# Turned rows moved beside the last tile of two attentions, and longer filling groups at three places, in a four-layer decoder kernel

## The reference, cut to what matters

```python
x = x + jnp.tanh(g_xattn[0]) * _L0_xattn_ref(_layernorm(x, axis=-1), ctx_1024, ctx_1024, ...)
x = x + jnp.tanh(g_ffn[0])   * _L0_ffn_ref(_layernorm(x, axis=-1), L0_ffn_router_w, ...)   # top-1 of 8 experts
x = x + jnp.tanh(g_xattn[1]) * _L1_xattn_ref(_layernorm(x, axis=-1), ...)
x = x + jnp.tanh(g_ffn[1])   * _L1_ffn_ref(_layernorm(x, axis=-1), L1_ffn_gate_w, ...)     # top-2 of 8 experts
x = x + ... # attention with causal scores; latent attention and top-2 experts
x = x + ... # rotary attention; one expert per batch, chosen from the last token
```

## Time and profile before

| | us |
|---|---|
| median of 3 runs | 1002.13 (1001.85 to 1003.92) |
| the profiled execution, its own time | 1003.53 |
| its span, first to last instruction | 1001.8 |
| PE busy (share of the span) | 905.4 (90%) |
| DVE busy | 729.6 (73%) |
| ACT busy | 551.0 (55%) |
| POOL busy | 431.4 (43%) |

### The profile page before, as it was taken

The page is one execution under the profiler, slowest core; times in us unless marked ns, Lnnn a source line. Parts: engine busy times, 40 slices in busy tenths (PEclk is TensorE's granted clock), DMA queues, the critical chain, the costliest instruction groups (busy, mean ns, idle before and its releaser), DMA issues.

```text
span 1001.8 us, 22263 instructions
## 1 busy us (share of the span) xinstructions
PE 905.4 (90%) x7859; PEld 629.1 (63%) x7863; DVE 729.6 (73%) x2035; ACT 551.0 (55%) x1331; POOL 431.4 (43%) x511
## 2 busy tenths in 40 slices
PE   5999887998798999889986898998989999989977
PEld 3777535667698999668774343434436777667764
DVE  5799998996786876789984776766734635479972
ACT  3786355883454556556642276766754243357743
POOL 5113555671265763645458657564531200022120
PEclk9899797997999999999999588989999999999999
DMA  9400000000211122300001322222002000000001
GB/s 334 165 2 3 3 5 1 2 2 1 59 47 40 44 47 76 119 0 1 0 1 55 87 64 82 62 79 58 26 1 106 2 1 1 1 1 3 2 2 43
DMA packets 29829, 40.75 MB, mean 41 GB/s; under 512 B 11456, under 2 KB 25024, under 8 KB 29216
## 3 DMA queue, kind: packets, MB, share of 16 engines
q1 hardware_dynamic: 27232, 34.28, 10.9%
q0 software_dynamic: 2496, 5.16, 2.0%
HBM read 31.45 MB, written 7.82 MB: 39 GB/s over the span
## 4 chain that ended last, share of the span: by engine, by line
PE 37%; issue 7%; POOL 6%; DVE 4%; ACT 3%; SPq 1%; DMA 0%; DVEq 0%; POOLq 0%; ACTq 0%
PE ps L922 5%; PE ps L912 5%; PE ps L1315 5%; PE ps L1287 4%; POOL att L1926 4%; PE ps L1299 4%; PE ps L831 2%; PE ps L840 1%; PE ps L843 1%; PE ps L816 1%; PE ps L1367 1%; PE ps L821 1%; PE ps L1375 1%; PE ps L770 1%; SPq L581 1%
## 5 line engine op out<-in xcount | busy, mean ns | idle before, releaser
L1907 POOL TENSOR_TENSOR rstd<-ve,minus_half 128x4 f32<-128x4 f32 x38 | 39.1, 1036 | 124.1 <-DVE ve L2214 107.5
L2860 DVE CUSTOM_DVE_ANT_0 U<-ps,cmaskb 128x384 bf16<-128x384 f32 (+1 forms) x128 | 53.9, 421 | 43.7 <-PE ps L1287 43.5
L2860 DVE CUSTOM_DVE_ANT_0 C<-ps,cmaskb 128x512 bf16<-128x512 f32 (+1 forms) x128 | 71.0, 555 | 20.1 <-PE ps L1287 17.2
L922 PEld LDWEIGHTS ps<-U,att 128*128 128x128 f32 x512 | 66.4, 191 | 30.4 <-issue 26.3
L1006 PE MATMUL ps<-PT,att 128*128 128x128 f32 x624 | 80.2, 283 | 4.6 <-issue 3.2
L2522 DVE SCALAR_TENSOR_TENSOR U<-ps,w_all,U 128x128 f32<-128x128 f32 x128 | 36.0, 344 | 62.1 <-PE ps L922 62.0
L1006 PEld LDWEIGHTS ps<-PT,att 128*128 128x128 f32 x624 | 75.2, 197 | 8.1 <-issue 5.6
L1577 ACT ACTIVATE att<-ps 128x512 f32<-128x512 f32 x64 | 38.1, 597 | 72.9 <-PE ps L912 72.8
L1299 PE MATMUL ps<-U,W 108*128 108x512 bf16 (+3 forms) x256 | 73.5, 327 | 5.0 <-ACT VW L1837 2.1
L1287 PE MATMUL ps<-W,U 72*128 72x512 bf16 (+3 forms) x256 | 67.7, 340 | 9.9 <-DVE VBD L2860 6.4
L922 PE MATMUL ps<-U,att 128*128 128x128 f32 x512 | 67.6, 276 | 0.6 <-ACT att L1577 0.6
(11 more groups left out here) (471 smaller groups left out, 2471.3 us busy)
## 6 DMA issues: line engine op xcount, KB each, us to landing
U<-in_ffn SPq DMA_DIRECT2D x1, 6176.0 KB, 23.0
U<-split SPq DMA_DIRECT2D x144, 32.0 KB
W<-split SPq DMA_DIRECT2D x144, 32.0 KB
W<-in_packed SPq DMA_DIRECT2D x1, 2162.5 KB, 22.4
U<-in_ffn SPq DMA_DIRECT2D x1, 2060.0 KB, 9.1
U<-in_moe SPq DMA_DIRECT2D x1, 2048.0 KB, 7.4
split<-VBD SPq DMA_DIRECT2D x4, 384.0 KB, 2.8
split<-W SPq DMA_DIRECT2D x4, 384.0 KB, 2.5
```

Of the source, the lines that this page charges most:

```text
L922: t = mm(ps[:, 4 + e % 2, i * D:(i + 1) * D], hh[:, u % 2, i * P:(i + 1) * P], W2M[:, e, j, :], start=(j == 0 and i == 0), stop=(j == J2 - ...
L2860: v.tensor_tensor_reduce(unused[t % 2][:, 0:z], ps[:, 2 * (t % RINGS), 0:z], visible[:, S - z:S], -1.0, -NEG, ALU.add, ALU.min, nm[:, n % ...
```

## The change

In X0 and X1 the rows of the first batches are normalised within the attention's loop (X0: batch 0 before the last `divide`, batches 1 and 2 behind it; X1: batches 0 and 1 before the last `divide`, 2 right behind it), and PE turns batch 0 in its loop behind the last weighted values, in place of filling products. Turned rows go through score banks, one for each of three batches, so that a turn doesn't wait for a copy. Behind the loop PE's order is route 0, turn 1, turn 2, route 1, route 2, ten filling products, turn 3, route 3, and PE and ACT no longer wait for all of x. Filling products in the attentions' tails: X0 17 + 13 before, 10 now; X1 6 + 26 before, none now; 10 more ahead of turn 3 in each. Filling groups elsewhere: `keep_warm` 7 to 9 turns (of eight) at the end of `dispatch` and 12 products more before the second slot's turn in `routed`; 8 to 12 turns in X3; in F3 10 products between L1355 and L1358, and 4 to 7 turns ahead of the experts.

```diff
-AHEAD = 2
+AHEAD = 3
+ROW_BANK = (0, 1, 2, 0)
...
         def turn_bank(s, b):
-            return 5 if s in (X0, F0, F1, MOE, F3) and b % 2 == 1 else 7
+            if s in (F0, F1):
+                return ROW_BANK[b]
+            return 5 if s in (X0, MOE, F3) and b % 2 == 1 else 7
...
+            def turn_row(s, b):
+                pe.wait_ge(s_xn, TB * (ROUND0[s] + b + 1))
+                if b == B - 1:
+                    turned_copied(s, 0)
+                for i in range(TB):
+                    t = pe.transpose(ps[:, ROW_BANK[b], i * P:(i + 1) * P], xn1[:, b * TB + i, 0:D], ident)
+                t.then_inc(turned, 1)
+
+            def other_rows(s, weight):
+                route(s, 0, weight)
+                turn_row(s, 1)
+                turn_row(s, 2)
+                route(s, 1, weight)
+                route(s, 2, weight)
+                warm(10, 3)
+                turn_row(s, B - 1)
+                route(s, B - 1, weight)
... PE, headwise
                     if s == X3 and k == 1:
-                        keep_warm(8)
+                        keep_warm(12)
...
-                    if k == NT + 2:
+                    if k == NT + 2 and s == X3:
                         warm(13, 0)
...
-                        if k == NT + 1:
+                        if k == NT + 1 and s == X0:
+                            pe.wait_ge(shifted, n0 + NT + 1)
+                            turn_row(F0, 0)
+                            warm(10, 3)
+                        elif k == NT + 1:
                             warm(17, 0)
... PE, dispatch and routed
-                keep_warm(7)
+                keep_warm(9)
...
                 for t in range(SLOTS + 2):
+                    if t == 1:
+                        warm(12, 7)
... PE, behind X0, and second_cross
-            prepare(F0, lambda b: route(F0, b, w("0rw")))
+            other_rows(F0, w("0rw"))
...
                     if k == NT + 3:
-                        warm(6, 0)
+                        pe.wait_ge(scores_read, NT + 1)
+                        turn_row(F1, 0)
                     if 0 <= k - 4 < NT:
                         turn_back(k - 4)
-                    if k == NT + 3:
-                        warm(26, 0)
...
-            prepare(F1, lambda b: route(F1, b, w("1gw")))
+            other_rows(F1, w("1gw"))
... PE, F3
             mm(ps[:, 6, 0:B], w("wp1"), FT[:, S - 1:B * S:S], start=True, stop=True).then_inc(pol, 1)
+            warm(10, 5)
             pe.wait_ge(pol_sb, 1)
...
-            keep_warm(4, bank=6)
+            keep_warm(7, bank=6)
... ACT: X0's loop, and behind X0 and X1
+                    if s == X0 and k == NT + 2:
+                        turned_copy(F0, 0, 0, [(FT[:, cols(0)], None, None)])
...
-            starts(act, F0)
-            for b in range(B):
+            for b in range(1, B):
...
-            starts(act, F1)
             for b in range(B):
... POOL, second_cross
-                    if 0 <= k - NT - 1 < EARLY:
-                        root(ROUND0[F1] + k - NT - 1, k - NT - 1)
+                    for b in {NT + 1: (0, 1), NT + 2: (2,)}.get(k, ()):
+                        root(ROUND0[F1] + b, b)
... DVE, headwise and second_cross
+                    if s == X0 and k == NT:
+                        normed_rows(F0, 0)
                 if s == X0:
-                    for n in range(AHEAD):
+                    for n in range(1, AHEAD):
                         normed_rows(F0, n)
...
-                    if 0 <= k - NT < EARLY:
-                        b = k - NT
+                    for b in {NT: (0, 1), NT + 1: (2,)}.get(k, ()):
                         dve.wait_ge(x_new, XNEW0[X1] + (b + 1) * TB)
                         moments(ROUND0[F1] + b, rows_of(x, b), b)
-                for n in range(AHEAD):
-                    normed_rows(F1, n)
+                    for b in {NT + 2: (0, 1), NT + 3: (2,)}.get(k, ()):
+                        normed_rows(F1, b)
```

## The result

The changed kernel took 993.52 us (median of 7 runs, 991.21 to 998.33) against 1002.62 for the kernel before beside it (7 runs, 1000.84 to 1004.70): ratio 0.9908 [0.9891, 0.9925], 9.1 us faster. The prediction said 997.5, from 994.0 to 1001.3: right in sign, too small, and the time lies just under the range.

What follows compares the result with a forecast made beforehand. Bound: PE's queue at half clock in the attention tails (F0's gate by only 0.64 us, then DVE). -0.6 - 2.4 - 0.4 - 1.0 + 0 + 0.3 - 1.9 = -6.0 from 1003.53: 997.5 us, range 994.0 to 1001.3.

Steps and rivals of the forecast that it cites:

- F0's gate: F0: one route instead of two queued behind the last turn, DVE becomes the bound, gate at about 109.7: -0.6 us.
- F1, gate and behind: F1: gate at about 240.7 with half clock from about 235.5, -2.4 us, and -0.4 behind the gate.
- fill before the slots: Before the slots: longer filling keeps the clock full at the slots' start: -1.0 us, between 0 and -1.7.
- X3's group: X3, ahead of the score: 32 more products fit PE's 2.44 us of idling, clock stays full: 0, at most +0.5.
- F3: F3: ten products between the policy products cost +0.3 us; full clock on the first experts' products saves 1.9.
- stages not touched: Stages the change leaves alone: no term in the sum; shifts there named only as a way of being wrong.
- The exponent's 0.4: Behind F1's gate: part of DVE's 0.94 us wait for the exponent goes, late projections and fillers set against it: -0.4 us.
- Rival 2: Clock falls at once in both tails for want of fillers: F0 +0.3, F1 -0.2, total 1001.0 us; chance 0.12.
- Turns and the clock: F3's earlier trace, nearly only turns with full clock behind, was taken to speak against the skill's rule on turns.
- Rival 3: F3's filling group becomes a wait if half clock begins before it, first experts 2.5 us later: 1006.1 us; chance 0.06.
- Rival 4: Clock falls in neither tail: F1's gate at 239.3, projections behind both gates at full clock: 994.2 us; chance 0.10.
- the last step of the sum: Whole kernel: the profiled execution's forecast of 997.5 us was set for the median too, 4.6 below its 1002.13.

Runs made afterwards that it cites:

- E8: Changed kernel with more filling products in both attention tails and 20 products in the fourteenth slot: 993.19 us, ratio 0.9892.
- E11: The same kernel as E8, run again: 991.93 us, ratio 0.9896.
- E13: Changed kernel with 20 products in the fourteenth slot and more filling in F1's tail, F0's tail as changed: 992.20 us, ratio 0.9903.
- E3: Kernel before with one dead DVE reduction, 1.35 us, ahead of F1's gate: 1001.36 us, ratio 0.9979.
- E4: Changed kernel with one dead DVE reduction, 2.02 us, ahead of F1's gate: 996.76 us, ratio 0.9943.
- E5: Changed kernel itself, no edit, run and profiled again: 995.87 us, ratio 0.9932.
- E10: Changed kernel with X3's first filling group back from 12 to 8 turns: 995.34 us, ratio 0.9922, 5 runs.
- E2: Kernel before with the longer filling groups alone (X3, before the slots, F3), row work as before: 1000.02 us, ratio 0.9965.
- E1: Changed kernel with the filling groups as before, so the row work of both attentions alone: 997.61 us, ratio 0.9952.
- E9: Kernel before with X3's first filling group 12 turns instead of 8: 1001.60 us, ratio 0.9982.
- E12: Changed kernel with more filling in both tails, without the fourteenth slot's 20 products but with E8's moved wait for `gi_set`: 995.83 us, ratio 0.9920.
- E6: Kernel before itself, no edit, run and profiled again: 1001.67 us, ratio 0.9995.
- E14: Changed kernel itself, no edit, run and profiled a third time: 996.19 us, ratio 0.9931.
- E7: Kernel before with only the row work of X1 and F1 as changed: 999.10 us, ratio 0.9967.

## Why the prediction was wrong in size

Point by point, by the sum's own terms. "With" and "without" are means over all profiles that have and lack the edit, without E8 and E11 to E13 and, in F1, without the delayed E3 and E4:

| step | forecast | first profile | with - without, all profiles |
|---|---|---|---|
| F0's gate | -0.6 | -0.75 | -0.72 (always -0.75) |
| F1, gate and behind | -2.8 | -2.44 | -2.2 (-1.06 to -3.34) |
| fill before the slots | -1.0 | -1.33 | -0.9 |
| X3's group | 0 | 0 | -1.4 |
| F3 | +0.3 - 1.9 | -1.82 | -1.6 |
| stages not touched | 0 | -6.0 | no difference shown; -5.6 to +4.0 in 320-860 alone |

- *F0*: right, mechanism and size. DVE was the bound; the gate had no idle time before it. The gain is 0.1 over the bound of 0.64 that the text gave.
- *F1*: right in mechanism. The text placed the gate at 240.7 if the clock fell at 235.5 and at 242.9 if at 231. It fell at 233.5 in the first profile (gate 239.22, after an F1 that began 1.37 earlier) and at 231.1 in E5, where the gate gained 1.10 and not 0.2. The early fall was overpriced. The exponent's 0.4 did not come in the first profile. On the mean F1 gave 2.2 of the 2.8.
- *Rival 2*, the fall at once in both tails, happened in E5 and E10: half clock from 101.4 and 101.7 in F0, from 231.1 and 231.4 in F1. The want of fillers isn't shown to be the cause in F0: E2 and E3, which have the old tail, fell at 101.5 and 101.9, and the first and third profile of the changed kernel at 103.8 and 104.3. In F1 no profile with the old tail fell before 234.6. The price in the text was wrong as well. Its terms 3 x 1.71 + 1.07 + 2 x 0.87 from 100.5 come to 108.4 and not to 106.9 for turn 3; in E5, which was 1.1 ahead of the kernel before at this point, turn 3 started at 104.62 and waited for DVE's rows (0.20), not for PE's queue, and the gate came without idle time before it, so F0's gain stayed. E5, turn 3 and the gate of F0, then the gate of F1:

```profile
104.62 1.12 PE L647 MATMUL ps<-W,KBD 128*128 128x128 f32 x4 [0.20 <-DVE KBD L2256]
...
108.46 0.28 DVE L2456 TENSOR_TENSOR att<-ps,W 128x128 f32<-128x128 f32 x1
...
240.02 0.29 DVE L2471 COPY att<-ps 128x128 f32<-128x128 f32 x1 [5.27 <-PE ps L685]
```

- *Turns and the clock*: in the window 230.1 to 233.5 of the first profile PE was busy for 3.20 of 3.40 us, with turns and router products of 8 columns alone, and half clock followed. The Trainium skill ("TensorE: Matmul & The Clock Gate", Part 4) says that a turn doesn't count as a busy PE in the way a product does. This window agrees with it; the window of turns in the earlier trace rows, from which the prediction argued, with full clock behind it, does not. No run here decides it.
- *Fill before the slots*: about as priced, though part of it can come without the group: the entry was 0.8 ahead in E1 and E3 and 1.3 in E9, all with the old group. With the new one it was 1.3 ahead in all six profiles that the table counts, but only 0.6 to 0.8 in E8, E11 and E12, where half clock lay at 259 us.
- *F3*: right; the ten products cost nothing that shows. Rival 3's mechanism did appear once. In E13 half clock lay on the fillers, and the step gave 0.90 instead of 1.82:

```profile
963.46 4.91 PE L621 MATMUL ps<-identb 128*128 128x128 bf16 x56
968.21 1.94 PE L1403 MATMUL ps<-FT,att 128*128 128x512 f32 x4
```

- *Rival 4*, no fall in either tail: its 994.2 takes 0.9 off for the exponent's wait, of which the sum had taken 0.4 already and which was 0.94 in all; it should have been 994.6, and the low end of the range stands on it.

**The step that failed** is the X3 term: "The clock was full here and stays: 0. Bounds: +0.5 [...], and a few tenths less than nothing in runs where the clock fell." showed PE idle for 2.44 us behind 64 fillers. That was the sign, the same as at the slots, where I did price it; I let one profile's full clock overrule it. In five of six executions the clock fell there, and the loss is 0.85 to 2.1 us, no few tenths.

**The second failure** is the last step of the sum. "The median of the runs is 1.4 lower than the profiled one; [...] so I set the same 997.5 for the median": that took the whole difference of two draws off the gain. The changed kernel's terms by the last column add up to 6.8 us, from the median 1002.9 to 996.1. The 20 runs have 994.87 (mean 995.54), which the standard deviation of 3.1 allows. With X3 in and the 1.4 not taken off, the forecast would have been 1002.13 - 6.0 - 1.4 = 994.7.

**The draw.** The first seven runs were lower than the next thirteen (993.52 against 995.87 and 996.19); over all runs the two medians lie 8.0 us apart, so some 1.1 us of the 9.1 is luck, and 994.87 would have been inside the range. My range counted unknown terms of the change and nothing for the spread of the stages it leaves alone; the text named this only as a way of being wrong. It began with the reading of the earlier trace rows: "the rest is full" passed over the 8s at 25 to 50, 575 to 625 and 650 to 675 us, and the slices hide single stretches of 3.4 us, such as those from 271.0, 312.0, 434.9 and 516.8 us. Such stretches are what falls differently from one execution to the next. That the untouched stages took another course in each execution is shown by E5, E6 and E14. What sets where the first half-clock stretch begins (19.5 to 22.6 us in sixteen profiles) stays open.

## What to carry to other kernels

When the clock drops in short stretches, one profile is one draw: profile the same kernel two or three times before pricing a dip, or its absence, at a place where PE waits (2.44 us in X3, 2.6 us in the fourteenth slot). Give every such place a chance of the fall and its price, and don't go by whether the clock happened to fall there once. And compare a new version stage by stage on the instructions of the bounding engine: F0 gave its 0.75 us in every profile that has the edit and F3 its 1.8 in all but one, F1 anything from 1.1 to 3.3 by the table above, and the stages that the change leaves alone moved by as much as the whole gain.

## What the hardware showed that I had not expected

- The same instructions from 320 to 860 us took from 5.6 us less to 4.0 us more than in the first profile, by where half clock fell.
- Half clock can last long on work that another execution runs at full clock: 23.9 us behind X2 in E14, without a break, on work that had 3.4 us of it in the first profile of the kernel and none in E5. That the slower products themselves held the clock down is a reading that no run tests.
- 1.4 us of dead work on the bounding chain cost nothing that can be measured (E3, 0.9979 [0.9959, 0.9998]); in its profile 0.89 of it was back by 262 us.
- The changed kernel's times spread wider than the old one's: standard deviation 3.1 against 1.7 us. E2 and E7, with a part of the change each, have 3.5. No experiment was made on why.
